# A graph network on one core: edge DMAs and weight pieces reordered on GpSimd, low halves on VectorE

## The reference, cut to what matters

```
xn = layernorm(x)
# layer 0
h   = xn @ gnn_W.T + gnn_b                       # messages along 20000 edges
gnn = segment_sum(norm * h[col], row)
q, k, v = split(xn @ W_qkv)                      # 16 heads of 64
attn = relu(q @ k.T * scale);  o = attn @ v      # no softmax
mix  = layernorm(o, gamma, beta) @ W_out + b_out
x = x + gnn + mix;   x = x + ffn(layernorm(x))
# layer 1: relational graph convolution, linear attention, 8 experts with top 2
#   the experts' weights W1 (8,1024,256) and W2 (8,256,1024) are used at the very end
```

## Time and profile before

| | |
|---|---|
| median of 3 runs | 2232.85 us (2232.0 to 2233.85) |
| profiled execution, its own time | 2239.03 us |
| its span in the trace | 2237.2 us |
| busy: TensorE | 2075.2 us, 93% |
| busy: VectorE | 1227.4 us, 55% |
| busy: GpSimd | 1052.9 us, 47% |
| busy: ScalarE | 754.6 us, 34% |
| the attention of layer 0 with its products | 18 to 685 us of the span |

### The profile page before, as it was taken

The page is one execution under the profiler, slowest core; times in us unless marked ns, Lnnn a source line. Parts: engine busy times, 40 slices in busy tenths (PEclk is TensorE's granted clock), DMA queues, the critical chain, the costliest instruction groups (busy, mean ns, idle before and its releaser), DMA issues.

```text
span 2237.2 us, 41143 instructions
## 1 busy us (share of the span) xinstructions
PE 2075.2 (93%) x16448; PEld 1420.5 (63%) x16448; DVE 1227.4 (55%) x2235; ACT 754.6 (34%) x1095; POOL 1052.9 (47%) x798
## 2 busy tenths in 40 slices
PE   7989989899899999979999999999999998976997
PEld 6445455455447977744445577757887787864765
DVE  6793453454477789984633632545655543284332
ACT  5253453453464454430031422412222221052332
POOL 3408777878775420014611783029433522433554
PEclk9999999999999999979999999999999999987999
DMA  4301332332356320041100012301211122376886
GB/s 158 91 7 40 86 75 51 86 75 60 81 142 143 128 88 20 21 167 43 38 1 29 22 46 76 99 28 39 69 40 40 40 43 62 137 282 191 154 152 108
DMA packets 128119, 182.14 MB, mean 81 GB/s; under 512 B 52065, under 2 KB 97256, under 8 KB 121678
## 3 DMA queue, kind: packets, MB, share of 16 engines
q1 hardware_dynamic: 111102, 150.87, 22.0%
q0 software_dynamic: 16848, 28.90, 7.7%
HBM read 120.82 MB, written 53.49 MB: 78 GB/s over the span
## 4 chain that ended last, share of the span: by engine, by line
PE 69%; POOL 11%; DVE 6%; issue 6%; ACT 2%; DMA 0%; DVEq 0%; POOLq 0%; SPq 0%; ACTq 0%
PE ps L494 17%; PE ps L497 17%; PE ps L496 17%; POOL edges_sorted L1536 4%; DVE RB L797 2%; PE pt L716 2%; PE pt L911 2%; PE ps L698 1%; POOL WR L1523 1%; POOL WR L1522 1%; POOL WR L1519 1%; PE pt L479 1%; PE ps L1173 1%; PE ps L1175 1%; PE ps L1174 1%
## 5 line engine op out<-in xcount | busy, mean ns | idle before, releaser
L494 PE MATMUL ps<-WR,RB 128*128 128x256 f16 (+2 forms) x2248 | 630.1, 280 | 6.4 <-DVE SR L1828 2.9
L497 PE MATMUL ps<-WR,RB 128*128 128x256 f16 (+2 forms) x2248 | 629.8, 280 | 0.0
L496 PE MATMUL ps<-WR,RB 128*128 128x256 f16 (+2 forms) x2248 | 629.7, 280 | 0.0
L494 PE MATMUL ps<-RB,WR 128*128 128x512 f16 (+1 forms) x720 | 246.6, 343 | 8.6 <-DVE RB L446 7.4
L494 PEld LDWEIGHTS ps<-WR,RB 128*128 128x128 f16 x2248 | 220.2, 98 | 51.7 <-DVE RB L446 3.1
L1472 POOL TENSOR_TENSOR WR<-WR,units 128x3072 f32<-128x3072 f32 (+2 forms) x16 | 74.2, 4634 | 371.5 <-PE ps L494 317.3
L497 PEld LDWEIGHTS ps<-WR,RB 128*128 128x128 f16 x2248 | 220.0, 98 | 42.5 <-issue 0.7
L497 PE MATMUL ps<-RB,WR 128*128 128x512 f16 (+1 forms) x720 | 246.4, 342 | 0.0
L496 PE MATMUL ps<-RB,WR 128*128 128x512 f16 (+1 forms) x720 | 246.3, 342 | 0.0
L496 PEld LDWEIGHTS ps<-WR,RB 128*128 128x128 f16 x2248 | 220.5, 98 | 39.9 <-issue 0.8
L1536 POOL DMA_INDIRECT edges_sorted<-SR x160 | 188.9, 1181 | 57.4 <-issue 57.4
(11 more groups left out here) (349 smaller groups left out, 4021.7 us busy)
## 6 DMA issues: line engine op xcount, KB each, us to landing
WR<-in_w_moe SPq DMA_DIRECT2D x64, 256.0 KB, 3.6
moe_split<-WR SPq DMA_DIRECT2D x128, 128.0 KB, 1.8
RB<-moe_split SPq DMA_DIRECT2D x8, 2048.0 KB, 15.6
WR<-in_w_mix SPq DMA_DIRECT2D x12, 1024.0 KB
WR<-in_w_mix SPq DMA_DIRECT2D x8, 1536.0 KB
RB<-in_x SPq DMA_DIRECT2D x18, 512.0 KB, 6.1
WR<-in_w_out SPq DMA_DIRECT2D x8, 1024.0 KB
RB<-counts SPq DMA_DIRECT2D x10, 640.0 KB, 4.9
```

The lines of the kernel that those rows point to most:

```text
L494: m = nc.tensor.matmul(o, ah, bh, start=(k == 0), stop=False)
L496: nc.tensor.matmul(o, ah, bl, start=False, stop=False)
L497: m = nc.tensor.matmul(o, al, bh, start=False, stop=(k == n - 1))
```

## The change

It has three parts.

1. **Low halves.** `weights_high` writes the high half only and signals `w_high` once; the scaling in place (L601) is gone. The low halves of slots 2 to 19 are all made by VectorE, in one operation (`weights_low`), and VectorE waits for `w_high` in its own order: after the third product tile in each slot of values or of queries and keys, after the third tile of pair 0 for slot 2, and in `gnn0` at blocks i = 0, 3, 6, 8, right after `z_ready` and ahead of that block's `g_sum`.
2. **Edge DMAs.** In a loop over p = 1 to 6, GpSimd waits until the first slot of the stage of products ahead of attention p has begun, and then issues 30, 16, 34, 17, 34 and 29 edge DMAs, one after the other.
3. **Pieces.** Behind the edge DMAs of stage p follow the pieces of batch p+1. The batches are 4, 9, 9, 9, 9, 9 and 15 pieces (5, 7, 9, 7, 10, 14 and 12 before); the first stands ahead of the loop.

```diff
         def weights_high(act, n):
             act.wait_ge(slot_begun, n)
             act.wait_ge(w_loaded, 16 * n + 16)
-            w = wst[:, 0:2048]
-            nc.scalar.activation(wh[n % 2][:, 0:2048], w, ACT.Copy, scale=WS).then_inc(w_high, 1)
-            act.wait_ge(w_high, 2 * n - 3)
-            nc.scalar.activation(w, w, ACT.Copy, scale=WS).then_inc(w_high, 1)
+            nc.scalar.activation(wh[n % 2][:, 0:2048], wst[:, 0:2048], ACT.Copy, scale=WS).then_inc(w_high, 1)
+        def weights_low(dve, n):
+            dve.wait_ge(w_high, n - 1)
+            nc.vector.scalar_tensor_tensor(wl[n % 2][:, 0:2048], wst[:, 0:2048], WS, wh[n % 2][:, 0:2048], ALU.mult,
+                                           ALU.subtract).then_inc(w_split, 1)
...
         def v0_dve(dve, d, T, beside=None):
             for i in range(NT):
                 v0_dve_one(dve, d, T, i)
+                if i == 2:
+                    weights_low(dve, 3 * d + 1)
...
         def qk0_dve(dve, p, T, beside=None):
             for t in range(6):
                 qk0_dve_one(dve, p, T, t)
+                if t == 2:
+                    weights_low(dve, 3 * (p // 2) + 2 + p % 2)
...
-        PIECE_END = {0: 0, 1: 5, 2: 12, 3: 21, 4: 28, 5: 38, 6: 52, 7: PIECES}
-        AFTER_SLOT = {5: 2, 6: 3, 8: 4, 9: 5, 11: 6}
+        PIECE_END = {0: 0, 1: 4, 2: 13, 3: 22, 4: 31, 5: 40, 6: 49, 7: PIECES}
+        MOVED = (0, 30, 46, 80, 97, 131, ET)
...
-            for n in range(2, 12):
-                low_part(n)
-                if n == 2:
-                    for k in pieces_of(1):
-                        piece(k)
-                if n == 4:
-                    pool.wait_ge(e_pos, 1)
-                    pool.wait_ge(e_clear, 16)
-                for t in range(max(n - 4, 0) * ET // 8, max(n - 3, 0) * ET // 8):
+            for k in pieces_of(1):
+                piece(k)
+            pool.wait_ge(e_pos, 1)
+            pool.wait_ge(e_clear, 16)
+            for p in range(1, PAIRS - 1):
+                pool.wait_ge(slot_begun, (3 * p + 4) // 2 + 1)
+                for t in range(MOVED[p - 1], MOVED[p]):
                     g.indirect_dma_start(edges_d, bass.IndirectOffsetOnAxis(pos[:, t:t + 1], 0),
                                          rec[:, t, :], None).then_inc(e_moved, 16)
-                if n in AFTER_SLOT:
-                    for k in pieces_of(AFTER_SLOT[n]):
-                        piece(k)
-            low_part(12)
-            for k in pieces_of(PAIRS - 1):
-                piece(k)
+                for k in pieces_of(p + 1):
+                    piece(k)
...
             gain(1)
-            low_part(13)
             for i in range(2, NT):
                 scale(i)
                 gain(i)
-                if i in (4, 7, 9):
-                    low_part(13 + i // 3)
...
             qk0_dve_one(dve, 0, T0, 2)
+            weights_low(dve, 2)
...
                 v.tensor_tensor(zz, zz, bcast[1], ALU.add).then_inc(z_ready, 1)
+                if i in (0, 3, 6, 8):
+                    weights_low(dve, 13 + (i + 1) // 3)
```

More of the change, by code:

```diff
@@ L597, in weights_high @@
             act.wait_ge(w_loaded, 16 * n + 16)
-            w = wst[:, 0:2048]
-            nc.scalar.activation(wh[n % 2][:, 0:2048], w, ACT.Copy, scale=WS).then_inc(w_high, 1)
-            act.wait_ge(w_high, 2 * n - 3)
-            nc.scalar.activation(w, w, ACT.Copy, scale=WS).then_inc(w_high, 1)
-        def high_only(act, n):
-            act.wait_ge(slot_begun, n)
-            act.wait_ge(w_loaded, 16 * n + 16)
             nc.scalar.activation(wh[n % 2][:, 0:2048], wst[:, 0:2048], ACT.Copy, scale=WS).then_inc(w_high, 1)
+        def weights_low(dve, n):
+            dve.wait_ge(w_high, n - 1)
+            nc.vector.scalar_tensor_tensor(wl[n % 2][:, 0:2048], wst[:, 0:2048], WS, wh[n % 2][:, 0:2048], ALU.mult,
+                                           ALU.subtract).then_inc(w_split, 1)
         def v0_act(act, d, T):
@@ L1280, in _ @@
                 if st - 1 in (OUTS_AT[0], OUTS_AT[NT], OUTS_AT[2 * NT]):
-                    high_only(act, 17 + OUTS_AT.index(st - 1) // NT)
+                    weights_high(act, 17 + OUTS_AT.index(st - 1) // NT)
             T0, r0 = TILE0["agg0"], TURN0["agg0"]
@@ L1523, in piece @@
                 g.tensor_tensor(psl[s], pst[s], psh[s], ALU.subtract).then_inc(pw_split, 1)
-            def low_part(n):
-                pool.wait_ge(w_high, 2 * n - 2)
-                split_low(n % 2, 2048)
-            for n in range(2, 12):
-                low_part(n)
-                if n == 2:
-                    for k in pieces_of(1):
-                        piece(k)
-                if n == 4:
-                    pool.wait_ge(e_pos, 1)
-                    pool.wait_ge(e_clear, 16)
-                for t in range(max(n - 4, 0) * ET // 8, max(n - 3, 0) * ET // 8):
+            for k in pieces_of(1):
[5 more added lines that the diff above has]
+                for t in range(MOVED[p - 1], MOVED[p]):
                     g.indirect_dma_start(edges_d, bass.IndirectOffsetOnAxis(pos[:, t:t + 1], 0),
                                          rec[:, t, :], None).then_inc(e_moved, 16)
-                if n in AFTER_SLOT:
-                    for k in pieces_of(AFTER_SLOT[n]):
-                        piece(k)
-            low_part(12)
-            for k in pieces_of(PAIRS - 1):
-                piece(k)
+                for k in pieces_of(p + 1):
+                    piece(k)
             pool.wait_ge(b_loaded, 32)
@@ L2011, in add_rows @@
                 v.tensor_tensor(rows, rows, rw[st % 4], ALU.add).then_inc(b_free, 1)
[L2012 to L2015, removed]
             hot(1)
@@ L2030, in _ @@
                 if st - 3 in (OUTS_AT[0], OUTS_AT[NT], OUTS_AT[2 * NT]):
-                    low_of(17 + OUTS_AT.index(st - 3) // NT)
+                    weights_low(dve, 17 + OUTS_AT.index(st - 3) // NT)
             dve.wait_ge(b_free, NST)
```

## The result

The changed kernel takes **2210.0 us** (median of 4 runs, 2207.77 to 2210.83), the kernel before on the same chip 2232.43 us (4 runs, 2227.72 to 2233.85): ratio 0.9902, 95% interval 0.989 to 0.9913, a gain of 22.4 us. The profiled execution took 2209.47 us, its span is 2207.7 us. Comparisons leave disturbed executions out, the longest of them one of 3629 us with a granted clock of 0.555 (in the experiment with the queue refilled).

A forecast was written before the change was run, and what follows sets the result against it. Beside TensorE, busy throughout the products, edge DMAs were taken to lengthen attentions 1 to 5. Terms 22.2 + 3.8 + 0.8 − 1.6 − 1.0 = 24.2 us gave 2208.6 us, with an 8 in 10 range of 2202 to 2220.

The forecast's parts named there:

- Part 1: Attentions 1 to 5: moving edge DMAs out saves 26.7 us, less 4.5 for those left inside, gain 22.2 us.
- Rival A: Attentions: edge DMAs are not the cause of their length, only 3.0 us gained, 2229.9 us; chance 5%.
- Part 2: GpSimd's regrouped pieces stay hidden behind the attentions, the last batch ending with 3.7 us in hand.
- Part 3: Low halves on VectorE: gains of 3.8 and 0.8 us, a loss of 1.6 at slot 13, otherwise hidden.
- The shift: Edge arithmetic before attention 0: VectorE's 125×40 operation no longer held 4.03 us by GpSimd's slot 3 low half, gain 3.8 us.
- +0.8: Products of p = 5: TensorE no longer waits for a low half GpSimd made behind its pieces, gain 0.8 us.
- Slot 13 (−1.6): Start of `gnn0`: VectorE's low half ahead of `g_sum` delays TensorE's next bank, loss 1.6 us (0 to 2.3).
- Rival B: Tail: late GpSimd delays slot 13's load, VectorE waits and TensorE stops; 2214.4 us, up to 2221; chance 15%.
- Holds of the port (−1.0): Stages of products: VectorE's low halves may hold GpSimd's DMAs over the shared port, loss 1 us (0 to 3.6).

The follow-up runs named there:

- the queue refilled: Changed kernel with eight pieces subtracting their low half five times instead of once, work nobody waits on: 2241.53 us, ratio 1.0055.
- second profile of before: The kernel before, profiled again with no edit: 2227.90 us.
- third profile: The kernel before, profiled a third time with no edit: 2230.59 us.
- part 3 alone: Kernel before with only the low halves moved to VectorE, edge DMAs and pieces in their old order: 2209.99 us, ratio 0.9916.
- the first profile: The kernel before, unedited, in the profile the prediction was read from: profiled execution 2239.03 us.
- slot 3 alone: Kernel before with only slot 3's low half subtracted by VectorE instead of GpSimd: 2227.97 us, ratio 0.9993.
- The better tail: Changed kernel with SyncE loading slot 13 and the `gnn0` bias earlier, and slot 13's low half behind the second `g_sum`: 2203.74 us, ratio 0.9888.

## Why the prediction was right in its number and wrong in its cause

2208.6 us were forecast, 2210.0 measured. The gain comes from elsewhere than the forecast said, and that the two sizes agree is luck: 22.2 us for a term that is worth nothing, and 18.3 us where 0.8 were forecast.

**What bounded the kernel.** GpSimd's groups from the places to the last piece, in the second profile of before (161 to 677.3, 516.3 us) and then after (161 to 655.2, 494.2 us); the columns are busy us, mean ns, and idle time just before the group:

```profile
L1536 POOL DMA_INDIRECT edges_sorted<-SR x160 | 188.9, 1181 | 56.0 <-issue 56.0
L1523 POOL TENSOR_TENSOR WR<-WR 128x512 f16<-128x512 f32 x58 | 67.0, 1156 | 4.5
L1519 POOL TENSOR_TENSOR WR<-WR,units 128x512 f32<-128x512 f32 x59 | 61.4, 1041 | 33.4 <-DMA WR<-in_w_moe 32.9
L1522 POOL TENSOR_TENSOR WR<-WR,units 128x512 f16<-128x512 f32 x59 | 61.3, 1039 | 4.6
L1479 POOL TENSOR_TENSOR WR<-WR 128x2048 f16<-128x2048 f32 x9 | 36.6, 4072 | 57.9 <-ACT WR L601 57.8
```

```profile
L1532 POOL DMA_INDIRECT edges_sorted<-SR x158 | 197.4, 1249 | 60.2 <-issue 55.1 <-PE ps L494 5.1
L1524 POOL TENSOR_TENSOR WR<-WR 128x512 f16<-128x512 f32 x60 | 69.4, 1157 | 4.7
L1520 POOL TENSOR_TENSOR WR<-WR,units 128x512 f32<-128x512 f32 x60 | 62.4, 1040 | 36.8 <-DMA WR<-in_w_moe 36.5
L1523 POOL TENSOR_TENSOR WR<-WR,units 128x512 f16<-128x512 f32 x60 | 62.4, 1039 | 4.7
```

In the first, DMAs with their pauses 244.9, pieces with their waits 232.2 and low halves 36.6 make 513.7 of 516.3 us. The 57.8 us of waiting before L1479 are one wait for ScalarE's scaled tile that began ahead of the stretch and ends 3 us into it. From there on GpSimd waits for no engine: it is full.

The queue ends 22.1 us earlier after the change. Some 12 of these stand ahead of the first edge DMA (168.3 and 156.2 us): the places are ready 3.2 us earlier, and GpSimd no longer waits 5 us for slot 4's scaled tile nor spends 4.1 us on its low half. From the first DMA to the end of the last piece it is 510.2 and 500.2 us: eight low halves leave, 32.5 us, but the edge DMAs are 11 us longer, waits for a stage's begin add 5.1, the pieces' loads 3.6 and one more piece 3.3. The kernel becomes 22.4 us faster by its medians; that this is so near 22.1 says little, as the profiled spans differ by 18.4.

**Part 1 (+22.2 us): wrong, and this is the step that failed.** "So 26.7 us go with 95 DMAs" rested on attentions of 42 to 45 us; they were a property of that one execution. In the second and third profile and in part 3 alone, attentions with 14 to 25 edge DMAs last 37.8 us. The forecast noted the danger itself ("I take it as a correlation"), and took GpSimd's share of the chain, 11% in the earlier trace rows (21% in the second profile), only as a warning. The same sum over GpSimd's rows would have shown a full queue in the first profile too, as its groups from 161 to 684.2 show: the same work, and 3.1 us more before L1479.

```profile
L1536 POOL DMA_INDIRECT edges_sorted<-SR x160 | 188.9, 1181 | 57.4 <-issue 57.4
...
L1479 POOL TENSOR_TENSOR WR<-WR 128x2048 f16<-128x2048 f32 x9 | 36.7, 4074 | 61.0 <-ACT WR L601 61.0
```

There the slow attentions hid it: TensorE came late by itself to where it would have waited (that this is the reason follows from these rows and has no run of its own).

**Rival A** was right that the edge DMAs aren't the cause, but gave 3.0 us. The rule set beside it, of the Trainium skill (SBUF — State Buffer, SBUF: two separate sides), that DMAs and engines can't contend, agrees with the 37.8 us of the attention with 18 DMAs.

**Part 2 (0): wrong in its size.** The last batch ended 6.6 us after the attentions instead of 3.7 before them. From the start of the last stage of products, the attentions end after 102.3 us instead of 106.3, since they are shorter than the forecast had them; the DMAs end after 47.7 instead of 45.0 and the 15 pieces take 61.2 instead of 57.6.

**Part 3.** The shift: +3.8 forecast; attention 0 fell by 51.35 − 47.21 = 4.1 us, though alone it is paid back (slot 3 alone: nothing). The products of p = 5: the mechanism of the "+0.8" was right and its size was not, 70.58 − 52.27 = 18.3 us against usual executions, 16.4 of them the wait itself, and the rest an estimate of what the lower clock behind it cost. Slot 13 (−1.6): its own delay was hidden in the changed kernel, where TensorE stood still only 0.57 us behind the transposes, and came out only when the bias was there in time. The span behind the attentions grew by 1557.9 − 1552.0 = 5.9 us: 3.7 of them TensorE's longer wait at the transposes for the late bias, while the 2.2 that are left fall in the stretch of lower clock and have no experiment of their own. The better tail takes the span behind the attentions to 1551.3. Rival B had a late GpSimd and a late load behind it right, at a price inside its range; that it was the bias, and not slot 13, it had wrong.

**Holds of the port (−1.0): they came, and were larger.** In the changed kernel eight of the nine low halves in the stages met an edge DMA, which took 2.05 to 2.99 us instead of 1.18 and ended some 1.05 us after VectorE's operation; the ninth fell into a pause of the DMAs. One of the eight:

```profile
189.84 2.28 DVE L603 SCALAR_TENSOR_TENSOR WR<-WR 128x2048 f16<-128x2048 f32 x1
190.76 2.41 POOL L1532 DMA_INDIRECT edges_sorted<-SR  x1 [0.30 <-issue]
```

That is 11.1 us of GpSimd's time in all; no DMA of the kernel before takes over 1.4 us. The stages of products do not show it, 51.9, 52.3 and 52.3 us against 53.0, 53.6 and 70.6, but the end of the queue does: without the holds the last piece would have ended, by an estimate that leaves the pieces' loads alone, 4 us before the attentions instead of 6.6 after them.

**The sum as measured**, second profile of before to after: attention 0 −4.1, products of p = 1, 3, 5 and what follows −1.1, −1.3, −18.3, −0.3; the first attention began 1.0 later, the tail took 5.9 more: −18.2, the spans differ by 18.4. Against the medians this is 4 us short, since the single executions stand within 2225 to 2235 us.

**Open:** why ScalarE began late and marks are missing in the first profiled execution, and whether the edge DMAs had a part in it in that one execution. No second such execution is among the other profiles.

## What to carry to other kernels

Before costing an edit to a helper engine, add up its rows from its first input to its last consumer, pauses and load waits included: if they fill the stretch, the engine is the bound, and a single wait removed elsewhere only moves to the next place that needs it. Not every microsecond taken off comes back: nine low halves less (36.6 us) brought the end of the queue 22 us forward, one less (4.1 us) did nothing, as waits for loads grew. And ask whether the work, once moved, holds up the helper from where it now stands. A stage that is slow in one profile and correlates with something is not a cause until a second profile of the same kernel shows it. When the helper is relieved, look at what its end releases: here loads at the end of SyncE's queue, the bias of `gnn0` above all, took back some 6 us, and moving two loads and one low half gave these back.

## What the hardware showed that was not expected

- Two executions of one program, 2239 and 2228 us, spent their time in different places: attentions of 42 to 45 us and products of 53 in one, of 37.8 and 70.6 in the other.
- 36 VectorE operations with both inputs in SBUF went from 381 to 810 ns beside GpSimd's 128x512 operations of 1.04 to 1.16 us, while those with a PSUM input stayed at 1.22 us.
- It works the other way too: an indirect DMA's issue on GpSimd went from 1.18 to 2.05 to 2.99 us beside a VectorE operation of 128x2048 with both inputs in SBUF, eight times out of eight, and ended 1.05 us after it.
- Waits of TensorE cost more than their length: behind one of 16.4 us the granted clock was 0.62 for 4.6 us, behind one of 6.4 us it was 0.50 for 3.3 us.
